# A four-layer block on one core: order of the scan's ramp, zero products for TensorE, earlier gates and weights, three experts first on one batch

## The reference

```python
x = x + attention(layernorm(x))        # 16 heads of 8, RoPE, softmax over 1024 keys
x = x + fp4_ffn(layernorm(x))          # blockwise fp4 of x, weights, hidden; silu(gate) * up; down
x = x + scan(layernorm(x))             # below
x = x + experts(layernorm(x))          # below

# scan: 128 channels x 32 states
dt = softplus(x @ dt_w.T + dt_b);  A = -exp(log_A)
b = x @ B_w.T + B_b;  c = x @ C_w.T + C_b
h = exp(A * dt_t) * h + (dt_t * x_t) * b_t      # step by step over 1024 tokens
y = sum over states of h * c_t  +  D_skip * x_t

# experts: 8, hidden 512; the two with the largest logits count
logits = x @ gate_w;  topk_vals, topk_idx = top_k(logits, 2);  gates = softmax(topk_vals)
out = sum over e of comb[:, e] * (gelu(x @ w1[e] + b1[e]) @ w2[e] + b2[e])
```

## Time and profile before

| | us |
|---|---|
| median of three runs | 928.56 |
| the profiled execution, its own time | 928.61 |
| its span from first to last instruction | 926.8 |
| PE busy | 777.1 (84%) |
| DVE busy | 791.6 (85%) |
| ACT busy | 689.2 (74%) |
| POOL busy | 238.5 (26%) |

### The profile page before, as it was taken

How to read it: one execution, slowest core, us unless ns; L and a number is a source line. 1 busy time by engine, 2 the same in 40 slices (tenths; PEclk the granted TensorE clock), 3 DMA queues, 4 the chain that set the end, 5 groups by cost and what they waited for, 6 DMA issues and landing times.

```text
span 926.8 us, 12582 instructions
## 1 busy us (share of the span) xinstructions
PE 777.1 (84%) x4288; PEld 409.2 (44%) x4288; DVE 791.6 (85%) x752; ACT 689.2 (74%) x1301; POOL 238.5 (26%) x134
## 2 busy tenths in 40 slices
PE   4689999999999999988666556676758787999998
PEld 3312212222122122224564355555757575888886
DVE  5998998898888899997996999999999664788774
ACT  2407888888788788786456996999986766888884
POOL 4800000000000000010010468997859301222100
PEclk9959999999999999999778789999889998999999
DMA  4313233221123110020003054464443303211111
GB/s 133 100 34 99 65 91 94 78 74 53 30 83 99 40 40 12 13 84 0 1 1 96 9 202 154 164 220 168 178 140 137 93 1 115 69 69 69 46 46 46
DMA packets 41324, 75.16 MB, mean 81 GB/s; under 512 B 7573, under 2 KB 25309, under 8 KB 40493
## 3 DMA queue, kind: packets, MB, share of 16 engines
q1 hardware_dynamic: 41260, 74.36, 25.2%
HBM read 64.71 MB, written 8.31 MB: 79 GB/s over the span
## 4 chain that ended last, share of the span: by engine, by line
PE 46%; DVE 26%; ACT 14%; issue 10%; POOL 2%; DMA 1%; DVEq 0%; ACTq 0%; POOLq 0%
PE ps L1640 9%; PE ps L1667 8%; DVE nmax_k L1211 7%; ACT dtb L1043 7%; PE ps L1927 6%; PE ps L1928 6%; PE ps L1929 6%; PE ps L1611 4%; ACT abar L1017 3%; DVE nmax L1208 3%; DVE hst L1377 2%; POOL hc L831 1%; PE ps L1801 1%; ACT prob L904 1%; DVE fx L506 1%
## 5 line engine op out<-in xcount | busy, mean ns | idle before, releaser
L904 ACT ACTIVATE prob<-ps 128x512 f32<-128x512 f32 x512 | 272.6, 599 | 92.4 <-PE ps L1640 90.5
L1211 DVE TENSOR_REDUCE nmax_k<-ps 128x2 f32<-128x1024 f32 x224 | 262.4, 1219 | 31.2 <-PE ps L1611 29.9
L831 POOL TENSOR_TENSOR hc<-hst,cbr 128x1024 f32<-128x1024 f32 x63 | 152.9, 2450 | 41.7 <-DVE hst L1377 21.4
L1640 PE MATMUL ps<-qs,ks 96*128 96x512 bf16 x512 | 159.8, 388 | 4.3 <-ACT prob L904 2.9
L1377 DVE TENSOR_TENSOR_SCAN hst<-abar,ps 128x1024 f32<-128x1024 f32 x64 | 143.1, 2274 | 5.7 <-PE ps L1827 2.9
L1667 PE MATMUL ps<-prob,vq 128*16 128x512 f32 x1024 | 136.3, 604 | 0.1
L1490 DVE TENSOR_TENSOR act_l<-act_t,act_h 128x1024 fp32r<-128x1024 f32 x64 | 86.3, 1361 | 39.0 <-ACT act_h L1139 39.0
L1043 ACT ACTIVATE dtb<-dtxt,bt 128x128 f32<-128x128 f32 x352 | 107.9, 406 | 0.9 <-PE ps L1827 0.9
L1135 ACT ACTIVATE act_t<-ps,b1t 128x512 f32<-128x512 f32 x128 | 81.8, 681 | 31.2 <-PE ps L1929 31.1
L1827 PE MATMUL ps<-ident,dtb 128*128 128x128 f32 x352 | 55.7, 301 | 57.3 <-DVE hst L1377 44.9
L1640 PEld LDWEIGHTS ps<-qs,ks 96*128 96x128 bf16 x512 | 34.0, 97 | 154.9 <-ACT prob L904 123.3
(11 more groups left out here) (213 smaller groups left out, 1089.7 us busy)
## 6 DMA issues: line engine op xcount, KB each, us to landing
cbr<-s_dram SPq DMA_DIRECT2D x64, 512.0 KB, 3.8
gate<-c_dram SPq DMA_DIRECT2D x6, 1024.0 KB, 4.7
qs<-q_dram SPq DMA_DIRECT2D x16, 288.0 KB
...
```

Source lines behind the costliest of these rows:

```text
L831: nc.gpsimd.tensor_tensor(hc[:, m % RING], hst[:, m % RING], cbr[:, m % RING], ALU.mult).then_inc(s_hc, 1)
L904: nc.scalar.activation(prob[:, n % 8], ps[:, 4 + (first + n) % 3], ACT.Exp, scale=ATT_SCALE).then_inc(s_exp, 1)
L1211: nc.vector.tensor_reduce(nmax_k[:, half, kk, 2 * pair:2 * pair + 2, qt], ps[:, 2 * pair:2 * pair + 2, :], AX.X, ALU.max, negate=True).the ...
L1640: nc.tensor.matmul(ps[:, 4 + (first + n) % 3], ks[p][:, kt // 4, j, kt % 4 * P:(kt % 4 + 1) * P], qs[p][:, half, j, :], start=True, stop=T ...
```

## The change

It has five parts.

1. **Zero products.** PE runs 14 products of zeros into a bank nobody reads before the weights are in, and 10 more after it has turned them.
2. **Order of the scan's ramp.** On ACT, exp(log_A), with its table, comes ahead of the copies of x; z of both chunks, |z| and exp go ahead of the two copies of c. The store of c for batch 1 leaves the head of SP's queue and comes after 16 rows have been issued.
3. **Softplus of batch 1.** Its u and ln u now lie in PSUM banks 4 and 5; `softplus_lost` follows `softplus_u` at once; ln, `softplus_dt`, `inflow_factor` and `b_rest` move by a step or so; ACT's `second_parts(1)` goes from step 14 to step 17.
4. **Gates and weights.** Batch 0's gates are finished inside the scan (exp at step 58, DVE at step 59, PE at step 62). Expert 2's weights are loaded at step 28, and POOL splits them right after expert 1's. The exp of batch 1's gates becomes a power of e on POOL.
5. **Unit order.** Three experts on batch 0 first (units 0 to 5), then the same three on batch 1 (6 to 11). Gates of expert 2 come in halves. The logits of batch 1 follow second_product(3), and combine(4) goes ahead of gates(1).

The diff, cut to its core:

```diff
-FIRST_UNITS = ((0, 0), (0, 1), (1, 0), (1, 1), (0, 2), (0, 3), (1, 2), (1, 3))
+EARLY = 3
+FIRST_UNITS = tuple((e, 2 * b + c) for b in range(BATCH) for e in range(EARLY) for c in range(2))
+        def grown(b):
+            return ps[:, 4:6].rearrange("p k t -> p (k t)") if b else dtx[:, 0:SEQ]
+        def logs(b):
+            return ps[:, 4:6].rearrange("p k t -> p (k t)") if b else ln_u[:]
...
 # SP
+            for m in range(BATCH * NSTATE):
+                if m == NSTATE // 2:
+                    store_c(1)
+                if m == NSTATE - 4:
+                    next_expert(2)
+                if m == NSTATE:
+                    sp.wait_ge(s_c_out[1], 16)
                 load_c(m)
...
             first_gates(0)
-            next_expert(2)
             next_expert(3)
+            sp.wait_ge(s_moe, 2 + FIRST_UNITS.index((0, 1)) + 1)
+            load_half_gate(2, 0)
             first_gates(1)
-            for e in range(2, EXPERTS):
+            next_expert(4)
+            sp.wait_ge(s_moe, 2 + FIRST_UNITS.index((0, 3)) + 1)
+            load_half_gate(2, 1)
+            for e in range(EARLY, EXPERTS):
 # POOL
-            pool.wait_ge(s_hc, BATCH * NSTATE)
+            pool.wait_ge(s_y3, BATCH * NSTATE - 2)
             upper_weights(2)
             lower_weights(2)
             norm_pool(3, 1)
+            pool.wait_ge(s_diff, 2)
+            nc.gpsimd.tensor_tensor(top[:, 3, 8:16], euler[:], top[:, 2, 8:16], ALU.pow).then_inc(s_ediff, 1)
 # ACT
             scale_act(2, 0)
+            nc.scalar.activation(a_neg[:], log_a[:], ACT.Exp).then_inc(s_a, 1)
             turn_act(2, 0)
             turn_act(2, 1)
             z_projected(0)
+            z_projected(1)
+            softplus_exp(0)
             c_projected(0)
-            z_projected(1)
             c_projected(1)
-            nc.scalar.activation(a_neg[:], log_a[:], ACT.Exp).then_inc(s_a, 1)
-            softplus_exp(0)
             softplus_ln(0)
...
-                if m == 14:
-                    second_parts(1)
                 if m == 16:
                     skipped(1)
+                if m == 17:
+                    second_parts(1)
-                if m == 60:
-                    second_gate(0)
+                if m == 58:
+                    second_gate()
+            turned_gates(0)
 # DVE
             softplus_u(1)
+            softplus_lost(1)
...
-                if m == 6:
-                    softplus_lost(1)
                 scan(m)
-                if m == 8:
+                if m == 9:
                     softplus_dt(1)
-                if m == 10:
+                if m == 11:
                     inflow_factor(1)
-                if m == 13:
+                if m == 12:
                     b_rest(1)
+                if m == 59:
+                    gates(0)
...
-            gates(0)
             add_scanned(1)
 # PE
+            def keep_running(count):
+                for n in range(count):
+                    nc.tensor.matmul(ps[:, 3], none_b[0:ROWS, 0:1].to_broadcast([ROWS, P]), blank, start=True, stop=True)
+            pe.wait_ge(s_fill, 1)
+            keep_running(14)
...
+            keep_running(10)
             turn_pe(0, 0)
+                if m == 62:
+                    turn_gates(0)
             first_product(0, (1,))
-            turn_gates(0)
             first_product(1)
+                second_product(m)
                 if m == 3:
                     logits(1)
-                second_product(m)
```

More of the change, by code:

```diff
@@ L292, in build_kernel @@
         s_u = sem("s_u")
+        s_lost = sem("s_lost")
         s_ln = sem("s_ln")
@@ L382, in last_unit, with gate_loads @@
             return max(m for m in range(UNITS) if unit_of(m)[0] == e)
+        def gate_loads(e, b):
+            if e < EARLY:
+                return ((1, 3), (1, 2), (2, 4))[e][b]
+            return e // 2 + (3 if e % 2 == 0 else 2)
         def turned_before(m):
@@ L724, in _, with next_expert @@
             load_expert(1, 1)
+            def next_expert(e):
+                sp.wait_ge(s_w_l, e - 1)
+                load_expert(e, e % 2)
             def load_c(m):
@@ L730, in load_c, with store_c @@
                 sp.dma_start(cbr[:, m % RING], s_dram[b, n:n + 1].to_broadcast([P, SEQ])).then_inc(s_c[m % RING], 16)
-            for b in range(BATCH):
+            def store_c(b):
                 if b:
@@ L737, in _, with load_half_gate @@
                 sp.dma_start(s_dram[b], bc32[0:NSTATE, 1, b * SEQ:(b + 1) * SEQ]).then_inc(s_c_out[b], 16)
-                if b == 0:
-                    sp.wait_ge(s_c_out[0], 16)
-                    sp.wait_ge(s_quant, HID_PIECE[3] + 1)
-                    for m in range(RING):
-                        load_c(m)
-            sp.wait_ge(s_c_out[1], 16)
-            for m in range(RING, BATCH * NSTATE):
+            store_c(0)
+            sp.wait_ge(s_c_out[0], 16)
+            sp.wait_ge(s_quant, HID_PIECE[3] + 1)
+            for m in range(BATCH * NSTATE):
[5 more added lines that the diff above has]
+                    sp.wait_ge(s_c_out[1], 16)
                 load_c(m)
+            def load_half_gate(e, b):
+                w = slice(b * SEQ, (b + 1) * SEQ)
+                sp.dma_start(gate[:, e % 2, w], c_dram[e:e + 1, w].to_broadcast([P, SEQ])).then_inc(s_gate[e % 2], 16)
             def first_gates(b):
@@ L780, in _ @@
             nc.gpsimd.memset(fill[:, 1], 1.0).then_inc(s_fill, 1)
+            nc.gpsimd.memset(euler[:], float(np.exp(1.0)))
             pool_step(nc.gpsimd.memset(expo[:], -0.5))
@@ L1000, in softplus_ln @@
             def softplus_ln(b):
-                w = slice(b * SEQ, (b + 1) * SEQ)
                 act.wait_ge(s_u, b + 1)
                 if b:
-                    act.wait_ge(s_dt, 2 * b)
-                nc.scalar.activation(ln_u[:], dtx[:, w], ACT.Ln).then_inc(s_ln, 1)
+                    act.wait_ge(s_lost, b + 1)
+                nc.scalar.activation(logs(b), grown(b), ACT.Ln).then_inc(s_ln, 1)
             def second_parts(b):
@@ L1087, in turn_and_round, with second_gate @@
                 nc.scalar.activation(xh[:, g * BANK:(g + 1) * BANK], ps[:, 4 + g % 2], ACT.Copy).then_inc(s_xh, 1)
-            def second_gate(b):
-                act.wait_ge(s_diff, b + 1)
-                nc.scalar.activation(top[:, 3, 8 * b:8 * b + 8], top[:, 2, 8 * b:8 * b + 8], ACT.Exp).then_inc(s_ediff, 1)
+            def second_gate():
+                act.wait_ge(s_diff, 1)
+                nc.scalar.activation(top[:, 3, 0:8], top[:, 2, 0:8], ACT.Exp).then_inc(s_ediff, 1)
             def turned_gates(b):
@@ L1330, in softplus_u @@
                 dve.wait_ge(s_e, 2 * b + 2)
-                nc.vector.tensor_scalar(dtx[:, w], dt[:, w], 1.0, None, ALU.add).then_inc(s_u, 1)
+                if b:
+                    dve.wait_ge(s_bc, BC_DONE[1])
+                nc.vector.tensor_scalar(grown(b), dt[:, w], 1.0, None, ALU.add).then_inc(s_u, 1)
             def b_rest(b):
@@ L1496, in combine @@
                 w = slice(c * BANK, (c + 1) * BANK)
-                dve.wait_ge(s_gate[e % 2], 16 * (1 + c // 2 if e < 2 else e // 2 + 2))
+                dve.wait_ge(s_gate[e % 2], 16 * gate_loads(e, c // 2))
                 dve.wait_ge(s_l2, m + 3)
@@ L1539, in _ @@
             second_parts(5)
+            combine(4)
             gates(1)
-            combine(4)
             for m in range(6, UNITS):
```

21 lines of the change are left out of this document (8 added, 13 removed).

## The result

The changed kernel takes 906.62 us (median of four runs, 906.17 to 909.79) against 928.59 before (926.12 to 929.52): ratio 0.9774, 95% interval 0.9749 to 0.9799. The prediction was 905.3, its own range 903 to 907.5. The profiled execution took 907.05 us, span 905.3, against 928.61 and 926.8.

What follows compares the result with a forecast made beforehand. PE's waits (13.2 us) and slow clock bound the experts' stage, DVE fed by ACT the scan. Gains 16.6 + 1.7 - 1.0 + 2.8 + 1.75 + 1.5 = 23.35 took 928.6 to 905.3 us, own range 903 to 907.5.

Steps and rivals of the forecast that it cites:

- Experts' stage, -16.6 forecast: Experts' stage: three PE waits and the slow clock behind two of them go, 4.7 + 1.4 + 2.2 + 6.3 + 2.0 us.
- units' order: Experts' stage, third wait: combine(4) no longer needs batch 1's gates; 6.3 us of wait and 2.0 of slow clock gone.
- exp 2.2: Experts' stage, second wait: with the exp on POOL, ACT neither waits nor reloads its table; 2.2 us gone.
- first wait: Experts' stage: batch 1's norm no longer waits behind expert 2's weights on POOL; 4.7 us and 1.4 of slow clock gone.
- Start of the experts' stage, -1.7 and +1.0: Unit 0: PE's wait for `comb` and its transposes go, 1.7 us; POOL's split delays DVE's act_l, 1.0 (bounds 0 to 3.0).
- 2.4 + 2.1 + 0.8 = 5.3: Scan: us gone from softplus exclusions (2.4), ACT's wait for `b_rest` reaching DVE (2.1), DVE's short waits for PE (0.8).
- The loss, counted at nothing: Scan: the 3.23 us loss row at 536.07 gains nothing, since ACT delivers abar no earlier.
- The gates term, +2.5: Scan: `gates(0)` enters where DVE has no gap, costing six operations and one exclusion, 2.5 us (bounds 1.3 and 5.7).
- Ramp, -1.75: Scan's ramp: z of chunk 1 to first_parts falls from 8.25 to 6.5 us, a gain of 1.75.
- Start, -1.5: Program start: zero products raise PE's clock, so DVE's chain starts 1.5 us earlier; bounds 1.7 gained or 1.0 lost.
- The part of 0.45 for the transposes: Program start: half of the first transposes lie ahead of ACT's first copy; 0.45 us gained at the faster clock.
- that of 1.07 for the products: Program start: three q and k products run at 606 ns instead of a mean of 961; 3 x 0.355 = 1.07 us gained.

Runs made afterwards that it cites:

- x5: Changed kernel with the first eight units in the old order and gates(1) ahead of combine(4) again; 916.11 us.
- x7: Changed kernel with batch 1's exp on ScalarE behind unit 4 again, instead of the power on GpSimd; 911.91 us.
- x11: Changed kernel with batch 0's gates behind the scan again and expert 2's weights issued behind those gates; 910.70 us.
- x4: Changed kernel with batch 0's gates computed and turned behind the scan again; 908.05 us.
- x3: Changed kernel with GpSimd's split of expert 1's weights at steps 30 and 35 of the scan instead of behind it; 909.57 us.
- x9: Changed kernel with expert 1's weights split at step 3 of the scan, and 18 + 1 zero products in place of the 10; 907.20 us.
- x12: Changed kernel with GpSimd's split of expert 1's weights at step 3 of the scan, its own start kept; 904.34 us.
- x6: Changed kernel with expert 2's weights issued behind batch 0's gates again, those gates staying in the scan; 904.80 us.
- x8: Changed kernel with softplus of batch 1 in SBUF as before, instead of PSUM; 911.59 us.

## Why the prediction was right, step by step

*Experts' stage, -16.6 forecast, -15.7 measured.* Right, and each term was found again when it was taken back: units' order 6.3 + 2.0 forecast, 8.3 measured (x5); exp 2.2, measured 3.1 (x7); first wait 4.7 + 1.4, measured 6.3 (x11 against x4). Their sum is 17.7. The 2.0 between that and 15.7 is the exclusion at act_l, which x3, x9 and x12 take away (184.9 to 182.8). One reason was incomplete: for the first wait I named only the early transfer, but moving gates(0) removes it as well (x6). Gates and weights together bought 1.1 to 1.5 us, not 4.3 (x11), because two prices were too low: 5.0 for 2.5 in the scan, and 2.0 for 1.0 at act_l.

*Start of the experts' stage, -1.7 and +1.0.* The first is right to the digit (9.86 to 8.13). The exclusions cost 2.0 to 2.1, not 1.0, and are paid behind second_product(0), in the last stretch; within the bounds of 0 to 3.0, but the reason for the lower end failed: both halves of act_l met an instruction of the split, and TensorE waited 1.6 us for the second half, which I had taken for covered. The other 1.1 us that x12 gains (8.13 to 7.05) is expert 1's split on hc(63), which the kernel before paid too.

*Scan.* The step of 2.4 + 2.1 + 0.8 = 5.3 was right in sum (5.0), and its parts are in the rows: the two softplus rows fell from 4.85 to 2.43 us, the wait of 2.06 for abar is gone, and of the 2.5 us of short waits for the transposes up to `lg` one of 1.2 is left (at 542.94). The loss, counted at nothing, fell by 2.0, but waits of 1.91 and 1.17 us stand in scans that follow it, where there were none; that is the reason the prediction gave (ScalarE delivers abar no earlier). These readings compare two profiles; x8 takes back only the two rows' place in memory, and at their new place. The gates term, +2.5, was mis-sized: +4.85 in the first profile, 5.0 by x11, 5.1 by x4. Its own rows cost 3.7, since two of them met an exclusion and I had counted one. Behind them VectorE's waits grew from 0.6 us (x11) to 1.8, all for TensorE, which now turns the gates there as well; these waits had no term. The choice of two ahead of them met an exclusion too (2.39 for a row of 0.23), but so it did before (2.40).

*Ramp, -1.75.* Right: -1.95, and 6.3 in every profile of the changed start order. 0.6 came back before the first scan row, where down(3)'s matmuls ran slower (5.49 us for 4.75).

*Start, -1.5.* The step "if the zero products raise the clock and it holds over some 2 us of idleness" failed in the profiled execution: it rose and did not hold. The profiles show both outcomes, which the bounds (-1.7 to +1.0) took in. The part of 0.45 for the transposes came (the products started 0.49 earlier); that of 1.07 for the products did not. The reading behind it, slow products under a clock row of 1.00, was right.

The Trainium skill, "TensorE: Matmul & The Clock Gate", section "What's actually happening", says that what the chip watches is free-running and does not reset when the kernel starts, so that the point at which the clock changes varies. The profiles agree: one start code, first rope rows from 17.57 to 19.23.

The profiled execution was 1.75 us over the forecast (907.05). The scan with its gates came out 2.7 us dearer, the start 1.7, and the FFN and ramp together 0.5, 4.8 in all with rounding; the 3.0 of attention, which the forecast did not have, paid for most of that. That was luck: the forecast was nearer than its terms were.
